# First layer's local attention: the second 128 queries in two halves with 128 keys each, two transposes a head, turned pairs in alternating PSUM banks

## The chip, the cores and the metric

The kernel runs on one core of one Trainium2 chip. The metric is the device time of one execution in microseconds (us). Before the change it is 3183.15 us, the median of 3 runs (3178.4 to 3184.4).

The core has a matrix engine (TensorE; PE in the rows, its weight loads PEld), a vector engine (VectorE, DVE), an activation engine (ScalarE, ACT), GpSimd (POOL) and a sync engine (SyncE, SP) that here issues the transfers. TensorE writes to PSUM, which has eight banks of 512 fp32 numbers in each of 128 partitions; everything else lies in SBUF.

## The reference

Two decoder layers over 8 sequences of 256 tokens with 512 features. Each layer has an attention (layer 0) or a state-space mixer (layer 1), a cross attention and a feed-forward block with experts. The change touches the local attention of layer 0 alone:

```python
q = q * cos + _rotate_half(q) * sin            # 16 heads of 32 features
k = k * cos + _rotate_half(k) * sin
scores = jnp.einsum('bhqd,bhkd->bhqk', q, k) * scale
rel = pos[:, None] - pos[None, :]
keep = (rel >= 0) & (rel < window)             # window is 64 for these constants
scores = jnp.where(keep[None, None], scores, -jnp.inf)
attn = jax.nn.softmax(scores, axis=-1)
out = jnp.einsum('bhqk,bhkd->bhqd', attn, v)
x = x + out.transpose(0, 2, 1, 3).reshape(B, S, EMB) @ w_out.T
```

A query sees itself and the 63 keys before it. Queries 0 to 127 need keys 0 to 127. Queries 128 to 191 need keys 65 to 191, and queries 192 to 255 need keys 129 to 255.

## The kernel before

`phase1` does the layer's two attentions, one sequence after the other (`for i in range(nseq)`). Each engine has one program, written out by hand, and it runs in the order in which it is written; engines wait for each other by semaphores (`due(name, i, k)` is the count of the k-th event of sequence i). There is no scheduler.

For a sequence, TensorE first computes queries and keys (`queries_keys`) and the values (`values(i, j)`, one for each 128 tokens j, into bank 6 + j). Then comes the stage that the change is about, here called the local stage. Heads go in pairs, n = 0 to 7, and a group c of four heads is two pairs. In program order TensorE does, for n = 0 to 11: `scores(i, n)` (n < 8), `values(i, 1)` (at n = 1), `turn_probs(i, n - 2)` (n = 2 to 9), and at n = 4, 6, 8, 10 `local_values` and `turn_recips` of group (n - 4) / 2. Right behind it stand `cross_values(0)` and the output projection.

- `scores` (L768 to L783): into two banks, one for each head of the pair, pair n using banks 0 and 1 or 2 and 3 in turn. First two bf16 matmuls lay the mask down (identity times `wmask_b`, 320 columns: 128 for the first 128 queries and `BAND` = 192 for the second); then the scores are added to it, 128 queries by keys 0 to 127 and 128 queries by keys 64 to 255. A head has 32 features, so the two heads lie on different 32-row strips of the array.
- VectorE takes the smallest (negated) score of each row for both blocks (L1047, L1048), ScalarE the exponentials with their row sums: for each head one of 128 and one of 192 columns (L669, L671), `scale=-1`, bias the smallest score. They go into `probs`, three buffers deep, where 64 zero columns lie between the two blocks.
- `turn_probs` (L785 to L794) transposes the pair's probabilities, 6 blocks of 128x128 (3 a head: queries 0 to 127 by keys 0 to 127, and queries 128 to 255 by keys 0 to 127 and 128 to 255), into bank 6 for one head and bank 7 for the other. From pair 1 on it waits until VectorE has copied the previous pair (`probsT_ready`), as every pair uses both banks; pair 0 waits until both value blocks have left those banks (`v_ready`).
- VectorE copies the 2 x 384 turned columns to `probsT` (L1055). `local_values` multiplies them with the values, four heads side by side on 32-column strips of the array: keys 0 to 127 with all 256 queries, then keys 128 to 255 with the second 128 queries, added. The reciprocals of the row sums are turned by `turn_recips`, copied by ScalarE (L619), and VectorE divides (L991).

SyncE's part in a sequence i >= 1 is, in its order: the value weights; the store of the sequence before (`normed_rows` and `mid`, 512 KB each, once VectorE has normalised its rows, which it does in the local stage at n = 2); the 2 MB of the cross-query weights (`load_unit(XQ)`); then those of the next sequence's queries.

Of the kernel before, what the change touches and what calls it, by code (L numbers as in the profile page):

```python
# [37 lines left out]
P = 128  # L38
# [16 lines left out]
BAND = S - P + WINDOW  # L55
# [26 lines left out]
wq_in w_hi w_lo slot_a slot_b colsT_lo hrT0_hi  # L82
# [251 lines left out]
def phase1(nc, sy, const, dr, held, nseq=NSEQ):  # L334
# [6 lines left out]
    with ExitStack() as ctx:  # L341
# [6 lines left out]
        wmask_b, ident_b = sb("wmask_b", [P, P + BAND], BF16), sb("ident_b", [P, P], BF16)  # L348
# [13 lines left out]
        wmask = arena[:, 2048:2048 + P + BAND]  # L362
# [4 lines left out]
        v, xv = sb("v", [P, NT, D]), held["xv"]  # L367
        probs = sb("probs", [P, 3, 2, P + S])
        probsT = arena[:, 0:3 * 2 * (P + S)].rearrange("p (b k s) -> p b k s", b=3, k=2)
# [75 lines left out]
        def _(sp):  # L445
# [11 lines left out]

            def load_raw(u, n, end, sem):
                first = raw_piece(u, n)
                sp.dma_start(first if end == n + 1 else flat[("w_sg", "w_su", "w_sd")[u]][:, n * D:end * D],  # L460
                             dr["w_units"][:, u, n * D:end * D]).then_inc(sy[sem], 16)
# [27 lines left out]
            for i in range(nseq):  # L489
                if i == 0:  # L490
                    for u in (K, V, XQ):
                        store_unit(u)
                else:
# [4 lines left out]
                    sp.wait_ge(sy["qk_proj"], due("qk_proj", i, 2 * KC))  # L498
                    load_unit(XQ)
# [34 lines left out]
        def _(pool):  # L534
            rstd_pool(pool, sy, norm_in(0), mv, ve, rstd, const["minus_half"])
            pool.memset(probs[:, :, :, P:P + WINDOW], 0.0).then_inc(sy["init1"], 1)
# [49 lines left out]
        def _(act):  # L586
# [65 lines left out]
            act.wait_ge(sy["init1"], 2)  # L652

            for i in range(nseq):
# [7 lines left out]
                for n in range(LPAIRS):  # L662
# [4 lines left out]
                    for k in range(2):  # L667
                        scores = bank_pair(2 * (n % 2))[:, k, :]
                        act.activation(probs[:, n % 3, k, 0:P], scores[:, 0:P], ACT.Exp, bias=smin[:, n, 0, k:k + 1],  # L669
                                       scale=-1.0, accum_out=ssum[:, c, 0, r + k:r + k + 1])  # L670
                        act.activation(probs[:, n % 3, k, P + WINDOW:P + S], scores[:, P:P + BAND], ACT.Exp,  # L671
                                       bias=smin[:, n, 1, k:k + 1], scale=-1.0,
# [40 lines left out]
        def _(pe):  # L713
# [54 lines left out]
            def scores(i, n):  # L768
# [27 lines left out]
            def local_values(i, c):  # L796
# [3 lines left out]
                for kt, (at, q0) in enumerate(((0, 0), (S, P))):  # L800
                    for r in range(HPC):
                        hh = c * HPC + r
                        n = hh // 2
                        ins = pe.matmul(bank(4 + c % 2)[r * HD:(r + 1) * HD, q0:S], v[:, kt, hh * HD:(hh + 1) * HD],
                                        probsT[:, n % 3, hh % 2, at:at + S - q0], start=(kt == 0), stop=(kt == 1),
# [58 lines left out]
            for i in range(nseq):  # L864
# [16 lines left out]
                if i == 0:  # L881
                    pe.wait_ge(sy["w1b_in"], n_late * 16)
                    pe.wait_ge(sy["ctx_in"], 16)
                    pe.wait_ge(sy["init1"], 2)
# [55 lines left out]
        def _(dve):  # L940
# [86 lines left out]
            for i in range(nseq):  # L1027
# [2465 lines left out]
```

## Time and profile before

| | |
|---|---|
| runs | 3183.15 us median (3178.4 to 3184.4) |
| profiled execution, its span | 3185.5 us (2.35 us above the median; no other time of its own is recorded) |
| TensorE matmuls busy | 2994.5 us, 94% |
| VectorE busy | 2329.6 us, 73% |
| ScalarE busy | 1588.2 us, 50% |
| GpSimd busy | 811.0 us, 25% |
| phase 1 (0 to 785 us): TensorE, VectorE, ScalarE busy | 712.58, 493.23, 283.75 us |
| the eight local stages, from the first mask to the first matmul behind the stage | 25.49 to 25.95 us each, 205.01 us in all |

A matmul's row holds its whole way through the array (a transpose of 128 columns reads 272 ns), and matmuls overlap: what one costs is the distance between the starts of two. Rows of the same line that follow each other are merged in the timeline (x6 are six instructions), and an fp32 matmul shows as two instructions, its two passes. "<-" names what ended the idle time ahead of a row.

### The profile page before, as it was taken

What the parts mean: (1) busy time and instruction counts of PE and PEld (TensorE: products, weight loads), DVE (VectorE), ACT (ScalarE), POOL (GpSimd) and SP (SyncE); (2) the same over time, 40 slices, a digit from 0 to 9 for tenths busy, and PEclk for the clock granted to TensorE, in tenths of its full rate; (3) what the DMA queues carried; (4) which work ended last, traced back from release to release, by engine and by line L of the source; (5) the groups of instructions that cost most, each with busy time, mean ns of one, the idle gap of its engine ahead of it and who ended that gap; (6) DMA issues with size and microseconds to landing.
All of it is one profiled execution on the core that took longest, in us unless ns stands there. A gap on an engine that the chain in (4) does not pass through costs nothing. (4 is left out here: it accounts for less than half of the span.)

```text
span 3185.5 us, 61039 instructions
## 1 busy us (share of the span) xinstructions
PE 2994.5 (94%) x22689; PEld 2409.3 (76%) x22689; DVE 2329.6 (73%) x4385; ACT 1588.2 (50%) x3643; POOL 811.0 (25%) x975
## 2 busy tenths in 40 slices
PE   7999999998999999999999959999999989999999
PEld 5665666665898888888888846767666678888888
DVE  5666666665875688888888767878785877777776
ACT  3333333334221455555555426666575766555555
POOL 1220221220664211111111063250603012222222
PEclk9999999999999999999999979999999999999999
DMA  6324323321231677777777741121200032222222
GB/s 271 112 87 167 133 106 120 117 83 47 82 95 34 199 246 238 251 238 250 242 241 247 245 144 57 58 87 35 80 25 31 18 131 79 76 77 74 76 77 70
DMA packets 145257, 401.85 MB, mean 126 GB/s; under 512 B 39232, under 2 KB 47936, under 8 KB 132240
## 3 DMA queue, kind: packets, MB, share of 16 engines
q1 hardware_dynamic: 106608, 323.30, 29.8%
q0 software_dynamic: 18976, 50.45, 5.5%
q10 hardware_dynamic: 19456, 25.18, 2.3%
q8 instruction: 140, 2.29, 0.3%
q14 instruction: 77, 0.63, 0.1%
HBM read 344.09 MB, written 54.76 MB: 125 GB/s over the span
## 5 line engine op out<-in xcount | busy, mean ns | idle before, releaser
L288 POOL DMA_INDIRECT hr<-normed_rows,idx x128 | 123.7, 966 | 634.5 <-PE psum L302 587.8
L3008 POOL TENSOR_TENSOR mixf<-act 128x256 f32<-128x256 f32 x128 | 143.2, 1119 | 458.3 <-DVE act L3274 458.3
L174 POOL TENSOR_SCALAR ve<-mv 128x1 f32<-128x1 f32 x112 | 35.8, 320 | 815.5 <-DVE mv L956 546.4
L328 PE MATMUL psum<-xT_hi,wgu_hi 128*128 128x192 f32 (+1 forms) x1536 | 227.9, 270 | 1.4 <-PEq L1117 0.8
L328 PE MATMUL psum<-xT_hi,wgu_lo 128*128 128x192 f32 (+1 forms) x1536 | 223.1, 267 | 0.0
L328 PE MATMUL psum<-xT_lo,wgu_hi 128*128 128x192 f32 (+1 forms) x1536 | 222.6, 267 | 0.0
L1734 ACT ACTIVATE eth<-psum 128x192 f32<-128x192 f32 (+1 forms) x192 | 63.2, 330 | 299.1 <-PE psum L328 294.3
L328 PEld LDWEIGHTS psum<-xT_hi,wgu_hi 128*128 128x128 f32 (+1 forms) x1536 | 189.8, 182 | 26.3 <-ACT wgu_hi L1718 21.5
L2302 ACT ACTIVATE scratch<-psum,smin 128x512 f32<-128x512 f32 x256 | 173.6, 686 | 59.9 <-DVE smin L2748 57.8
L328 PEld LDWEIGHTS psum<-xT_hi,wgu_lo 128*128 128x128 f32 (+1 forms) x1536 | 190.3, 182 | 0.0
L328 PEld LDWEIGHTS psum<-xT_lo,wgu_hi 128*128 128x128 f32 (+1 forms) x1536 | 190.2, 182 | 0.0
L2748 DVE TENSOR_REDUCE smin<-psum 128x2 f32<-128x1024 f32 x128 | 155.2, 1215 | 38.6 <-PE psum L2479 37.9
L3274 DVE TENSOR_TENSOR act<-act,maskT 128x512 f32<-128x512 f32 x128 | 88.1, 688 | 116.7 <-ACT act L3050 116.3
L2489 PEld LDWEIGHTS psum<-ident,scratch 128*128 128x128 f32 x1024 | 112.0, 143 | 56.7 <-issue 39.1
L2489 PE MATMUL psum<-ident,scratch 128*128 128x128 f32 x1024 | 148.0, 286 | 5.1 <-DVE scratch L2755 2.7
L1844 DVE SCALAR_TENSOR_TENSOR eact<-eth,psum 128x192 f32<-128x192 f32 (+1 forms) x192 | 67.4, 351 | 112.4 <-ACT eth L1734 110.0
L3284 DVE TENSOR_TENSOR ca_lo<-act,ca_hi 128x512 fp32r<-128x512 f32 x128 | 134.2, 1049 | 12.4
L1257 POOL DMA_INDIRECT slot_token<-tok_i,slot_w x96 | 105.8, 1102 | 66.7 <-DVE slot_r L1582 37.4
L723 PE MATMUL psum<-hT_hi,w_slot 128*128 128x256 f32 x768 | 111.3, 289 | 11.8 <-ACT hT_hi L600 5.9
L2116 POOL DMA_INDIRECT yk<-expert_out,slots x84 | 86.8, 1033 | 124.2 <-issue 49.5
L1088 DVE TENSOR_SCALAR arena<-psum,hi 128x512 f32<-128x512 f32 x128 | 87.5, 743 | 40.9 <-PE psum L826 40.8
L3063 ACT ACTIVATE ca_hi<-act 128x512 fp32r<-128x512 f32 x128 | 81.0, 633 | 66.5 <-DVE act L3274 66.5
(466 smaller groups left out, 8725.9 us busy)
## 6 DMA issues: line engine op xcount, KB each, us to landing
w_sg<-in_w_gu_dram SPq DMA_DIRECT2D x32, 1408.0 KB
w_su<-in_w_gu_dram SPq DMA_DIRECT2D x32, 1408.0 KB
w_slot<-w_split SPq DMA_DIRECT2D x21, 2048.0 KB
w_raw<-in_w_dram SPq DMA_DIRECT2D x128, 256.0 KB, 2.6
w_sd<-in_w_d_dram SPq DMA_DIRECT2D x32, 512.0 KB
wd<-in_w_d_dram SPq DMA_DIRECT2D x32, 512.0 KB
expert_out<-so ACTq DMA_DIRECT2D x64, 256.0 KB, 5.3
w_slot<-w_split SPq DMA_DIRECT2D x28, 512.0 KB
```

Source lines behind the costliest of these rows:

```text
L288: pool.indirect_dma_start(out=xg[0:w, t, :], out_offset=None, in_=rows, in_offset=bass.IndirectOffsetOnAxis(ap=idx[0:w, t:t + 1], axis=0)) ...
L328: ins = pe.matmul(bank(2 + m)[0:w, gu * CAP:(gu + 1) * CAP], wgu2[wp][:, gu, kc, m0:m0 + w], xT2[xp][:, kc, :], start=(i == 0 and kc == 0) ...
L723: ins = pe.matmul(out, lhs_of(lp, kc), rhs_of(rp, kc), start=(m == 0 and kc == 0), stop=(m == 2 and kc == KC - 1))
L1088: dve.tensor_scalar(xprobs[:, n % 4, kt], bank_pair(2 * (n % 2))[:, :, kt * S:(kt + 1) * S], hi[:, kt:kt + 1], -SCORE_CLIP * ROOT_HD, ALU. ...
L1257: pool.indirect_dma_start(out=dr["slot_token"], out_offset=bass.IndirectOffsetOnAxis(ap=slot_w[s % 2][:, j, k:k + 1], axis=0), in_=tok_i[s ...
L2116: pool.indirect_dma_start(out=gathered(s, NT * k + j), out_offset=None, in_=dr["expert_out"], in_offset=bass.IndirectOffsetOnAxis(ap=slots ...
L2302: act.activation(prob[:, q % 4, k, :], bank_pair(2 * (q % 2))[:, k, :], ACT.Exp, bias=smin[b][:, n, k:k + 1], scale=-1.0, accum_out=ssum[b ...
L2489: ins = pe.transpose(bank(4 + k)[:, mc * P:(mc + 1) * P], prob[:, q % 4, k, mc * P:(mc + 1) * P], ident)
L2748: dve.tensor_reduce(smin[(q // PAIRS) % 2][:, q % PAIRS, :], bank_pair(2 * (q % 2)), AX.X, ALU.min).then_inc(sy["smin_ready"], 1)
L3008: pool.tensor_tensor(mixf[:, g % LAG, :], act2[:, g % LAG, 0, :], act2[:, g % LAG, 1, :], ALU.add).then_inc(sy["f_mix"], 1)
L3274: dve.tensor_tensor(act2[:, g % LAG], act2[:, g % LAG], maskT[(g // FC) % 2][:, 2:4, :], ALU.mult).then_inc(sy["f_ca"], 1)
L3284: dve.tensor_tensor(ca2[1][:, g % LAG], act2[:, g % LAG], ca2[0][:, g % LAG].bitcast(F32), ALU.subtract).then_inc(sy["f_ca_lo"], 1)
```

## The change

The second 128 queries are taken in two halves. Queries 128 to 191 meet keys 64 to 191, queries 192 to 255 meet keys 128 to 255: 128 keys each, so that every row of scores has 128 columns in both blocks.

- Mask: 256 columns instead of 320. Scores: the second block's matmul of 128 queries by 192 keys becomes two of 64 queries by 128 keys, which write partitions 0 to 63 and 64 to 127 of the same columns (tile positions `(r0, 0)` and `(r0, 64)`).
- One reduction over both blocks instead of two; four exponentials of 128 columns a pair instead of two of 128 and two of 192. The zero columns in `probs` go.
- Four transposes a pair instead of six. Both heads of a pair fill one bank (6 for even pairs, 7 for odd), so `turn_probs` waits for the copy of the pair before last; pairs 0 and 1 wait for one value block each. The copy takes 512 columns instead of 768.
- `local_values`: per head one matmul of 128 columns and two of 64, nothing added. The middle half needs keys 64 to 191 on partitions 0 to 127, so SyncE copies the halves of two value blocks into a new tile `v_mid` (`shift_values`, two transfers of 64 rows of 2 KB within SBUF, once `v_ready` is complete). Group 0 waits for it (`vs_in`). In sequences 1 to 7 these transfers stand between the store and the cross-query weights, in sequence 0 ahead of the last weight store.

```diff
+            def shift_values(i):
+                sp.wait_ge(sy["v_ready"], due("v_ready", i, NT))
+                sp.dma_start(v_mid[0:HALF, :], v[HALF:P, 0, :]).then_inc(sy["vs_in"], 16)
+                sp.dma_start(v_mid[HALF:P, :], v[0:HALF, 1, :]).then_inc(sy["vs_in"], 16)
...
                     sp.wait_ge(sy["qk_proj"], due("qk_proj", i, 2 * KC))
+                    shift_values(i)
                     load_unit(XQ)
...
-                        act.activation(probs[:, n % 3, k, P + WINDOW:P + S], scores[:, P:P + BAND], ACT.Exp,
-                                       bias=smin[:, n, 1, k:k + 1], scale=-1.0,
+                        act.activation(probs[:, n % 3, k, P:S], scores[:, P:S], ACT.Exp,
+                                       bias=smin[:, n, k, 1:2], scale=-1.0,
...
-                    pe.matmul(bank_pair(2 * (n % 2))[:, k, 0:P + BAND], ident_b[:], wmask_b[:], start=True,
+                    pe.matmul(bank_pair(2 * (n % 2))[:, k, 0:S], ident_b[:], wmask_b[:], start=True,
                               stop=True)
                 c = n // 2
-                for q0, k0, at, width in ((0, 0, 0, P), (P, WINDOW, P, BAND)):
+                for p0, end, q0, k0, at in ((0, P, 0, 0, 0), (0, HALF, P, HALF, P), (HALF, P, P + HALF, P, P)):
                     for k in range(2):
-                        rows = slice((2 * (n % 2) + k) * HD, (2 * (n % 2) + k + 1) * HD)
-                        ins = pe.matmul(bank_pair(2 * (n % 2))[:, k, at:at + width], qk[rows, c, q0:q0 + P],
-                                        qk[rows, KC + c, k0:k0 + width], start=False, stop=True,
-                                        skip_group_check=True)
+                        r0 = (2 * (n % 2) + k) * HD
+                        rows = slice(r0, r0 + HD)
+                        ins = pe.matmul(bank_pair(2 * (n % 2))[p0:end, k, at:at + P], qk[rows, c, q0:q0 + end - p0],
+                                        qk[rows, KC + c, k0:k0 + P], start=False, stop=True,
+                                        tile_position=(r0, p0), skip_group_check=True)
...
-                if n >= 1:
-                    pe.wait_ge(sy["probsT_ready"], due("probsT_ready", i, n))
+                if n >= 2:
+                    pe.wait_ge(sy["probsT_ready"], due("probsT_ready", i, n - 1))
                 else:
-                    pe.wait_ge(sy["v_ready"], due("v_ready", i, NT))
+                    pe.wait_ge(sy["v_ready"], due("v_ready", i, n + 1))
                 for k in range(2):
-                    for b3 in range(3):
-                        ins = pe.transpose(bank(6 + k)[:, b3 * P:(b3 + 1) * P],
-                                           probs[:, n % 3, k, b3 * P:(b3 + 1) * P], ident)
+                    for t in range(NT):
+                        ins = pe.transpose(bank(6 + n % 2)[:, k * S + t * P:k * S + (t + 1) * P],
+                                           probs[:, n % 3, k, t * P:(t + 1) * P], ident)
...
+                if c == 0:
+                    pe.wait_ge(sy["vs_in"], 2 * 16 * (i + 1))
-                for kt, (at, q0) in enumerate(((0, 0), (S, P))):
+                for keys_of, q0, q1 in ((v[:, 0, :], 0, P), (v_mid[:], P, P + HALF), (v[:, 1, :], P + HALF, S)):
                     for r in range(HPC):
...
-                        dve.tensor_reduce(smin[:, n, 0, :], pair[:, :, 0:P], AX.X, ALU.min)
-                        dve.tensor_reduce(smin[:, n, 1, :], pair[:, :, P:P + BAND], AX.X, ALU.min
-                                          ).then_inc(sy["lmin_ready"], 1)
+                        dve.tensor_reduce(smin[:, n], pair[:, :, 0:S].rearrange("p k (t s) -> p k t s", t=NT), AX.X,
+                                          ALU.min).then_inc(sy["lmin_ready"], 1)
...
-                        dve.tensor_copy(probsT[:, m % 3], bank_pair(6)[:, :, 0:P + S]
+                        dve.tensor_copy(probsT[:, m % 3].rearrange("p k s -> p (k s)"), bank(6 + m % 2)
                                         ).then_inc(sy["probsT_ready"], 1)
```

On TensorE, before, from the scores of pair 4 to those of pair 5 (`wmask_b` is the mask, `qk` the scores, `probs` the transposes, `arena,v` the values, `recb` the reciprocals):

```order
L773 MATMUL psum<-wmask_b,ident_b 128x320 x2
L779 MATMUL psum<-qk 128x128 x2
L779 MATMUL psum<-qk 128x192 x2
L792 MATMUL psum<-ident,probs 128x128 x6
L804 MATMUL psum<-arena,v 32x256 x4
L804 MATMUL psum<-arena,v 32x128 x4
L812 MATMUL psum<-ident,recb 128x128 x2
L773 MATMUL psum<-wmask_b,ident_b 128x320 x2
L779 MATMUL psum<-qk 128x128 x2
```

The same place after the change:

```order
L779 MATMUL psum<-wmask_b,ident_b 128x256 x2
L786 MATMUL psum<-qk 128x128 x2
L786 MATMUL psum<-qk 64x128 x4
L799 MATMUL psum<-ident,probs 128x128 x4
L813 MATMUL psum<-arena,v 32x128 x4
L813 MATMUL psum<-arena,v_mid 32x64 x4
L813 MATMUL psum<-arena,v 32x64 x4
L821 MATMUL psum<-ident,recb 128x128 x2
L779 MATMUL psum<-wmask_b,ident_b 128x256 x2
L786 MATMUL psum<-qk 128x128 x2
```

The steps stand in the same order; two transposes and 64 mask columns are gone, the second scores are four matmuls on 64 output partitions, and the values are twelve matmuls with fewer columns.

On SyncE's queue, before, in sequence 2 (`w_slot_76` and `w_slot_77` are the two weight slots, `so` holds the rows stored):

```order
L468 DMA w_slot_76<-w_split 128x1024 x4
L455 DMA normed_rows<-so 128x2x512
L456 DMA mid<-so 128x1024
L468 DMA w_slot_77<-w_split 128x4096
L468 DMA w_slot_76<-w_split 128x4096
```

The same place after the change:

```order
L473 DMA w_slot_76<-w_split 128x1024 x4
L455 DMA normed_rows<-so 128x2x512
L456 DMA mid<-so 128x1024
L460 DMA v_mid<-v 64x512
L461 DMA v_mid<-v 64x512
L473 DMA w_slot_77<-w_split 128x4096
L473 DMA w_slot_76<-w_split 128x4096
```

The two new transfers stand behind the store's 1 MB and ahead of 4 MB of weights.

## Rows read from the trace of the kernel before

**Rows 1.** Busy time by stretch: sequence 2's local stage, and all eight

```profile
core 0: us, PE busy (x) PEld busy (x) DVE busy (x) ACT busy (x) POOL busy (x), PEclk, DMA share, GB/s
239.89:265.49 25.60, 22.65 (x213) 15.16 (x213) 19.64 (x40) 14.19 (x68) 0.19 (x1) 1.00 0.53 207
...
sum 205.01, PE 181.15 PEld 121.24 DVE 156.40 ACT 117.05 POOL 1.34; mean PE 22.64 PEld 15.15 DVE 19.55 ACT 14.63 POOL 0.17
```

**Rows 2.** Timeline of TensorE, sequence 2 (start, length, engine, line, operation, count, idle before)

```profile
246.63 0.85 PE L792 MATMUL psum<-ident,probs 128*128 128x128 f32 x6 [0.39 <-ACT v L613]
...
251.18 0.27 PE L792 MATMUL psum<-ident,probs 128*128 128x128 f32 x1
251.38 0.42 PE L804 MATMUL psum<-arena,v 128*32 128x256 f32 x4
251.38 0.86 PE L804 MATMUL psum<-arena,v 128*32 128x256 f32 x16
...
252.44 0.43 PE L773 MATMUL psum<-wmask_b,ident_b 128*128 128x320 bf16 x2
252.81 0.82 PE L779 MATMUL psum<-qk 32*128 32x128 f32 x8
253.56 0.87 PE L792 MATMUL psum<-ident,probs 128*128 128x128 f32 x6
254.27 0.43 PE L773 MATMUL psum<-wmask_b,ident_b 128*128 128x320 bf16 x2
...
256.35 0.86 PE L804 MATMUL psum<-arena,v 128*32 128x256 f32 x16
...
261.31 0.86 PE L804 MATMUL psum<-arena,v 128*32 128x256 f32 x16
```

**Rows 3.** Groups by line and shape in phase 1 (busy us, mean ns of one)

```profile
L1047 DVE TENSOR_REDUCE lmin<-psum 128x2 f32<-128x256 f32 x64 | 26.9, 420 | 35.5 <-PE psum L779 35.0
L1048 DVE TENSOR_REDUCE lmin<-psum 128x2 f32<-128x384 f32 x64 | 35.0, 547 | 0.0
L1055 DVE COPY arena<-psum 128x768 f32<-128x768 f32 x64 | 60.9, 951 | 13.7 <-PE psum L792 13.1
L1088 DVE TENSOR_SCALAR arena<-psum,hi 128x512 f32<-128x512 f32 x128 | 87.5, 743 | 40.9 <-PE psum L826 40.8
L669 ACT ACTIVATE probs<-psum,lmin 128x128 f32<-128x128 f32 x128 | 47.1, 368 | 60.3 <-DVE lmin L1048 60.1
L671 ACT ACTIVATE probs<-psum,lmin 128x192 f32<-128x192 f32 x128 | 54.0, 421 | 0.0
```

**Rows 4.** Timeline of ScalarE: first and last exponential of pair 5

```profile
254.59 0.37 ACT L669 ACTIVATE probs<-psum,lmin 128x128 f32<-128x128 f32 x1 [1.26 <-DVE lmin L1048]
...
255.99 0.21 ACT L671 ACTIVATION_READ_ACCUMULATOR probs<-psum,lmin 128x1 f32 x1
```

**Rows 5.** Groups by line and shape: weight loads of 128, 64 and 32 columns

```profile
L779 PEld LDWEIGHTS psum<-qk 32*128 32x128 f32 x64 | 4.2, 185 | 2.1 <-issue 2.1
L1791 PEld LDWEIGHTS psum<-wd,eact 128*64 128x64 f32 x12 | 0.8, 136 | 0.7 <-issue 0.4
L804 PEld LDWEIGHTS psum<-arena,v 128*32 128x32 f32 x512 | 13.4, 109 | 19.8 <-DVE arena L1055 10.3 <-issue 4.0
```

**Rows 6.** Sequence 2: the store's issue, its transfers to landing, the last value copy

```profile
244.58 0.37 SPq L455 DMA_DIRECT2D normed_rows<-so  x1
...
normed_rows<-so SPq DMA_DIRECT2D x1, 512.0 KB, 2.8
mid<-so SPq DMA_DIRECT2D x1, 512.0 KB, 4.1
...
245.85 0.63 ACT L613 ACTIVATE v<-psum 128x512 f32<-128x512 f32 x1
```

**Rows 7.** Busy time by stretch, layer 1: ahead of and in a stretch at half clock

```profile
2020.00:2028.00 8.00, 6.30 (x68) 4.05 (x65) 7.96 (x13) 5.22 (x14) 0.80 (x2) 1.00 0.01 3
2028.00:2038.00 10.00, 9.51 (x76) 6.95 (x80) 7.14 (x12) 4.31 (x12) 1.58 (x4) 0.50 0.00 0
```

More of the change, by code:

```diff
@@ L54 @@
 NEG = -1e30
-BAND = S - P + WINDOW
+HALF = P // 2
 LPAIRS = HEADS // 2
@@ L81 @@
 xattn_ready delta_psum delta_taken clip_bounds rs_ready shared_in init1 x_in ctx_in mask_in rows_out
-wq_in w_hi w_lo slot_a slot_b colsT_lo hrT0_hi
+wq_in w_hi w_lo vs_in slot_a slot_b colsT_lo hrT0_hi
 """.split()
@@ L347, in phase1 @@
         cosT, sinT = sb("cosT", [P, S]), sb("sinT", [P, S])
-        wmask_b, ident_b = sb("wmask_b", [P, P + BAND], BF16), sb("ident_b", [P, P], BF16)
+        wmask_b, ident_b = sb("wmask_b", [P, S], BF16), sb("ident_b", [P, P], BF16)
         bq, bk = sb("bq", [P, KC]), sb("bk", [P, KC])
@@ L361, in phase1 @@
         qk_raw = arena[:, 0:2 * KC * S].rearrange("p (c s) -> p c s", c=2 * KC)
-        wmask = arena[:, 2048:2048 + P + BAND]
+        wmask = arena[:, 2048:2048 + S]
         qk = sb("qk", [P, 2 * KC, S])
@@ L366, in phase1 @@
         swap = [p ^ 1 for p in range(HD)]
-        v, xv = sb("v", [P, NT, D]), held["xv"]
-        probs = sb("probs", [P, 3, 2, P + S])
-        probsT = arena[:, 0:3 * 2 * (P + S)].rearrange("p (b k s) -> p b k s", b=3, k=2)
+        v, v_mid, xv = sb("v", [P, NT, D]), sb("v_mid", [P, D]), held["xv"]
+        probs = sb("probs", [P, 3, 2, S])
+        probsT = arena[:, 0:3 * 2 * S].rearrange("p (b k s) -> p b k s", b=3, k=2)
         smin, ssum = sb("lmin", [P, LPAIRS, 2, 2]), sb("lsums", [P, KC, NT, HPC])
@@ L490, in _ @@
                 if i == 0:
-                    for u in (K, V, XQ):
+                    for u in (K, V):
                         store_unit(u)
+                    shift_values(0)
+                    store_unit(XQ)
                 else:
@@ L535, in _ @@
             rstd_pool(pool, sy, norm_in(0), mv, ve, rstd, const["minus_half"])
-            pool.memset(probs[:, :, :, P:P + WINDOW], 0.0).then_inc(sy["init1"], 1)
             sy.link(pool, "pool_link", pool.memset(one_hot[:], 0.0))
@@ L651, in _ @@
             cols_copy(turned_in(0))
-            act.wait_ge(sy["init1"], 2)
             for i in range(nseq):
@@ L668, in _ @@
                         scores = bank_pair(2 * (n % 2))[:, k, :]
-                        act.activation(probs[:, n % 3, k, 0:P], scores[:, 0:P], ACT.Exp, bias=smin[:, n, 0, k:k + 1],
+                        act.activation(probs[:, n % 3, k, 0:P], scores[:, 0:P], ACT.Exp, bias=smin[:, n, k, 0:1],
                                        scale=-1.0, accum_out=ssum[:, c, 0, r + k:r + k + 1])
-                        act.activation(probs[:, n % 3, k, P + WINDOW:P + S], scores[:, P:P + BAND], ACT.Exp,
-                                       bias=smin[:, n, 1, k:k + 1], scale=-1.0,
+                        act.activation(probs[:, n % 3, k, P:S], scores[:, P:S], ACT.Exp,
+                                       bias=smin[:, n, k, 1:2], scale=-1.0,
                                        accum_out=ssum[:, c, 1, r + k:r + k + 1]).then_inc(sy["probs_ready"], 1)
@@ L803, in local_values @@
                         n = hh // 2
-                        ins = pe.matmul(bank(4 + c % 2)[r * HD:(r + 1) * HD, q0:S], v[:, kt, hh * HD:(hh + 1) * HD],
-                                        probsT[:, n % 3, hh % 2, at:at + S - q0], start=(kt == 0), stop=(kt == 1),
+                        ins = pe.matmul(bank(4 + c % 2)[r * HD:(r + 1) * HD, q0:q1], keys_of[:, hh * HD:(hh + 1) * HD],
+                                        probsT[:, n % 3, hh % 2, q0:q1], start=True, stop=True,
                                         tile_position=(0, r * HD), skip_group_check=True)
@@ L883, in _ @@
                     pe.wait_ge(sy["ctx_in"], 16)
-                    pe.wait_ge(sy["init1"], 2)
+                    pe.wait_ge(sy["init1"], 1)
                     keys(0, range(KC))
@@ L3432, in host_layout @@
     q, k = np.arange(P)[:, None], np.arange(P)[None, :]
-    k1 = np.arange(WINDOW, S)[None, :]
+    k1 = np.where(q < HALF, k + HALF, k + P)
     keep = np.concatenate([(q >= k) & (q - k < WINDOW), (q + P >= k1) & (q + P - k1 < WINDOW)], 1)
```

## The prediction

> **What bounds the kernel now.** I read the busy time by stretch first. The eight local stages take 205.0 us of the 3185.5, each about 25.6, and in one of them no engine is full: of 25.60 us TensorE shows 22.65, VectorE 19.64, ScalarE 14.19 [rows 1]. So the stage is a chain that goes round between the engines, and the timeline of TensorE shows the ring. From one group's values to the next (251.38 to 256.35) are 4.97 us [rows 2]. TensorE's own steps in it, start to start: values and reciprocals 1.06 (251.38 to 252.44), scores 1.12 (252.44 to 253.56) and six transposes 0.71 (253.56 to 254.27), the last two twice: 4.72 us. The other 0.25 us is waiting for VectorE's copy, because every pair of heads uses both turned banks. So TensorE bounds the middle of the stage, VectorE and ScalarE its opening and its end, where there are no other scores to fill in.
>
> What the stage gives up reaches the end: the matmuls of cross values follow it at once and need nothing of it, and the profile shows no transfer that this part of phase 1 waits for.
>
> **The change part by part, on TensorE.**
>
> - Transposes: six take 0.87 us to the last one's end and one takes 0.27, so 0.12 us from start to start [rows 2]; two fewer turn the step's 0.71 us into 0.49.
> - Mask: two matmuls of 320 columns and one change of the array's tiling take 0.37 us (252.44 to 252.81) [rows 2]. The change of tiling is about 0.1: from the last transpose to the first values matmul are 0.20 us (251.18 to 251.38), of which 0.11 is the transpose's own streaming [rows 2]. So 0.13 us for 320 columns, 0.11 for 256: 0.05 us saved on two.
> - Scores: eight instructions in 0.75 us (252.81 to 253.56) [rows 2]. With 0.11 us for a pass of 128 columns and 0.16 for 192 these are two passes of each (0.54), a first weight load that nothing hides (0.11) and the change of tiling behind (0.1). After: two passes of 128 (0.22), another change of tiling, from 32x128 to 32x64 tiles (0.1), a load that is not hidden (0.05: the load of 64 columns takes 136 ns, between 185 for 128 and 109 for 32 [rows 5]), and, if the two halves run side by side, two passes of 128 (0.22) with 0.02 for issuing four tiles. With the first load and the last change as before that is 0.82 us, 0.07 more than before, and the mask gives 0.05 back. The step stays at 1.12 us: fewer columns, one more change. Bounds: 0.97 us if that change costs nothing, 1.33 if the halves run one after the other.
> - Values: before, passes of 256 and of 128 columns twice each, 0.64 us. After, two of 128 and four of 64: 0.44 if a pass of 64 costs half of one of 128, 0.66 if it costs as much. No row here has 64 columns on 32-column strips. I take 0.44, because what could hold a short pass up is its weight load, and that is the shortest one here [rows 5]: values and reciprocals 1.06 to 0.86 us.
>
> **On the other engines.** VectorE's two reductions take 420 ns (256 elements) and 547 (384), 1 ns an element; one of 512 is 0.67 us in place of 0.97. The copy of 768 takes 951 ns, of 512 by the same slope 0.69; the nearest row, another instruction on 512 columns, has 743 [rows 3]. ScalarE's four exponentials run from 254.59 to 256.20, 1.61 us [rows 4]; two get shorter by 421 less 368 ns [rows 3], so 1.50.
>
> **The walk through one stage** (sequence 2), with hand-overs between engines of about 0.1 us:
>
> - First mask to first values, 11.49 us before. Two pairs of scores, the second value block and the third scores are as they were. Pair 0's transposes no longer wait for the second value copy (0.39 us [rows 2]) and start at 246.2. The scores of pair 4 then wait for the exponentials of pair 2: 246.2 + 0.67 + 1.50 and hand-overs, 248.6. Adding 1.12 and 0.49, the values start at 250.2: 10.34 us.
> - First to second values: TensorE alone, 0.86 + 2 x (1.12 + 0.49) = 4.08 in place of 4.97. The copies are ready in time, because a pair now has a bank of its own.
> - Second to third values, 4.96 before (256.35 to 261.31): scores of pair 7 end 2.05 us after the start; reduction, copy and hand-overs add 1.45: 3.50. VectorE sets this.
> - Third values to the stage's end, 4.18 before (261.31 to 265.49): pair 7's transposes wait for its exponentials (0.94), then 0.63 to their end, copy 0.69, hand-overs 0.18, values and reciprocals 0.86: 3.30.
>
> Together 4.38 us. With before's durations the same walk comes out 0.2 short of the rows, so I count 4.2. Eight stages: 33.6 us. From the profiled execution's 3185.5 that is 3151.9; it lies 2.35 above the median, and from the median it is 3149.6.
>
> **The added wait.** Group 0's values wait for `v_mid`; behind them on TensorE stand the reciprocals and all later scores, and for those both other engines wait. The second value copy ends at 246.48 (245.85 + 0.63) [rows 6], about 0.5 us earlier after the change; two issues at 0.37 us follow. The store's transfers of 512 KB took 2.8 and 4.1 us from issue to landing [rows 6], the second behind the first. `v_mid` has 256 KB and queues behind that store, so 248.8 to 250.5 us against a need at 250.2: I cost it at nothing, with up to 0.3 us a stage. The cover is the opening; past it each us late is a us lost. The cross-query weights are moved behind it by about 1.4 us, and the output projection and more stand ahead of their first use.
>
> **A page's rule against the change.** The four column tiles of the values start together: four matmuls in 0.42 us, while their rows are 0.39 long [rows 2], all on the same 128 rows. The Trainium skill, in "TensorE: Matmul & The Clock Gate", Part 3 (what overlaps and what doesn't), says that a weight load overlaps running matmuls only when the row groups differ. By that rule the two halves of a head, which share their rows, would run one after the other, and the time would be the first rival's; the trace disagrees for 32-column tiles, and no run here shows 64-column tiles on 32 rows.
>
> **The rivals.**
>
> 1. The halves run one after the other: 0.21 us more for each of seven scores that TensorE waits for nothing else in, 1.5 a stage, 12 in all: 3162. For it: no row mixes row and column tiles. Against: each alone runs side by side [rows 2].
> 2. The third tiling costs no change: scores 0.97, about 1.3 us a stage more saved, 10.5 in all: 3139. "TensorEngine Tiling (Array Packing)", Key Properties, of the Trainium skill says that changing the tiling mode drains the engine; by it this rival falls, but no row shows these two modes side by side.
> 3. `v_mid` comes late. If its small packets are served mixed with the weights behind them (2 MB, at up to twice the stretch's mean 207 GB/s [rows 1] 5 us), it lands near 253.3, 3.1 us late in sequences 1 to 7: 22 lost, 3172. Against: the store's two transfers landed one after the other.
> 4. Slower: TensorE's clock falls in the stage. It is at 2.4 GHz in all eight [rows 1]. In layer 1 it fell to half for 10 us behind 8 us with 6.30 busy [rows 7], and the new stage streams fewer columns with more gaps. One such stretch in every stage doubles 5 us of steps: 8 x (5 - 4.2) = 6 us lost, 3190. It decides from 8.4 us at 1.2 GHz a stage; all of it would be far worse, above 3300. Against: TensorE's share of the stage hardly falls (4.08 of 4.08 in the middle).
> 5. The change doesn't do what it says: the new bank order still makes pairs wait, 0.5 us a stage: 3154, inside the forecast's own range.
>
> **How the numbers follow.** Forecast 0.67 (rival 5 in it), own range 3144 to 3156 (values not shorter costs 0.7 us a stage, a copy of 743 ns a little). Rival 1 0.12, rival 2 0.10, rival 3 0.06, rival 4 0.05. The range reaches over both tiling rivals, 3138 to 3164, and leaves out most of 3 and 4. About 0.2%, 6.4 us, is what a measurement of this kernel can tell from no change. Faster: 0.67 + 0.12 + 0.10 and half of rival 3, 0.92; same 0.04; slower 0.04, nearly all rival 4.
>
> **What would show it.** In the profile after: stages near 21.3 us; distance from first to second values near 4.1; the scores' second block starting about 0.4 us behind the first, its four matmuls within 0.03 us (right) or 0.2 apart (rival 1); 64-column passes 0.06 apart; one reduction of 0.67 and a copy of 0.69; no idle TensorE ahead of the first values; granted clock 1.00. The prediction is wrong if that first wait is over 1 us, or the clock row shows halves in a stage.

## The result, and the profile after

The changed kernel takes 3152.55 us, the median of 4 runs (3145.23 to 3157.93), beside 3183.78 us (3178.4 to 3188.07) for the kernel before on the same chip: 0.9906 of its time, 95% interval 0.989 to 0.9922, or 31.2 us less. The profiled execution has a span of 3156.0 us, 29.5 less than before's 3185.5. The forecast was 3150, with 33.6 us saved in the eight local stages. The total is near that; what the profile saves in the stages is not. Of six later runs of the changed kernel (below) one took 6928.04 us; nothing on record says why, and it is left out of every comparison.

The busy time by stretch for the eight local stages of the changed kernel, which answers to [rows 1] (columns as there; the granted clock, PEclk, is the third from the end, 1.00 being 2.4 GHz):

```profile
41.95:63.59 21.64, 20.07 (x261) 13.58 (x261) 15.24 (x31) 15.75 (x73) 0.00 (x0) 0.99 0.48 190
141.12:162.41 21.29, 19.86 (x260) 13.53 (x261) 15.85 (x32) 13.12 (x68) 0.19 (x1) 1.00 0.67 262
232.07:253.36 21.29, 19.86 (x260) 13.53 (x261) 15.84 (x32) 13.13 (x68) 0.19 (x1) 1.00 0.67 261
323.04:345.87 22.83, 21.41 (x261) 14.66 (x261) 15.84 (x32) 13.23 (x68) 0.19 (x1) 0.93 0.64 243
415.53:438.34 22.81, 21.39 (x261) 14.63 (x261) 15.85 (x32) 13.24 (x68) 0.19 (x1) 0.93 0.64 243
508.00:530.77 22.77, 21.34 (x260) 14.55 (x261) 15.85 (x32) 13.24 (x68) 0.19 (x1) 0.93 0.65 244
600.48:628.24 27.76, 25.65 (x260) 17.33 (x261) 16.12 (x32) 13.34 (x68) 0.19 (x1) 0.75 0.51 200
697.90:719.20 21.30, 19.88 (x261) 13.53 (x262) 15.83 (x32) 13.12 (x68) 0.19 (x1) 1.00 0.44 161
sum 181.69, PE 169.46 PEld 115.34 DVE 126.42 ACT 108.18 POOL 1.34; mean PE 21.18 PEld 14.42 DVE 15.80 ACT 13.52 POOL 0.17
```

Where the granted clock is 1.00 and nothing is late, here called an undisturbed stage, it takes 21.29 us in place of 25.60, 4.31 less. Sequences 3, 4 and 5 are 1.5 us longer at a mean clock of 0.93, and sequence 6 is 6.5 us longer at 0.75. So the stages save 205.01 - 181.69 = 23.3 us in this execution. All eight without those losses (7 x 21.29, and 21.64 for sequence 0) would take 170.7 and save 34.3.

The other 6.2 us of the span's 29.5 lie in layer 1, whose code is the same. Two stretches of it, each from the same matmul to the same matmul, before and after:

```profile
1800.10:2000.00 199.90, 157.15 (x1115) 116.93 (x1114) 141.65 (x272) 93.93 (x246) 86.42 (x110) 0.91 0.37 120
2200.00:2400.00 200.00, 189.07 (x1603) 139.17 (x1604) 153.47 (x278) 126.23 (x330) 63.75 (x91) 0.96 0.20 59
```

```profile
1776.70:1973.30 196.60, 157.20 (x1115) 117.22 (x1114) 142.73 (x272) 93.69 (x246) 86.07 (x110) 0.90 0.38 122
2173.30:2369.70 196.40, 185.96 (x1604) 136.71 (x1605) 153.59 (x278) 126.17 (x330) 64.08 (x92) 0.97 0.19 60
```

They are 3.3 and 3.6 us shorter after. In the second a higher granted clock goes with it (0.97 for 0.96); in the first none does, and the cause there is open. Such differences come from execution to execution: the four runs above lie 12.7 us apart. From the first matmul behind phase 1 (transposes of `hr`) to the end are 2419.8 us before and 2413.4 after in these two profiles, and 2409.0 and 2409.6 in a second profile of each kernel (below, taken on two different chips). In that second pair the span is 31.1 us shorter, all of it in phase 1, which ends 31.8 us earlier.

An undisturbed stage, sequence 2 from the first to the last local values, on the timeline of TensorE (columns as in [rows 2], to which it answers):

```profile
242.53 0.43 PE L813 MATMUL psum<-arena,v 128*32 128x128 f32 x8
242.77 0.29 PE L813 MATMUL psum<-arena,v_mid 128*32 128x64 f32 x8
242.88 0.29 PE L813 MATMUL psum<-arena,v 128*32 128x64 f32 x8
243.11 0.44 PE L821 MATMUL psum<-ident,recb 128*128 128x128 f32 x2
243.38 0.38 PE L779 MATMUL psum<-wmask_b,ident_b 128*128 128x256 bf16 x2
243.69 0.87 PE L786 MATMUL psum<-qk 32*128 32x128 f32 x12
244.49 0.66 PE L799 MATMUL psum<-ident,probs 128*128 128x128 f32 x4
244.99 0.38 PE L779 MATMUL psum<-wmask_b,ident_b 128*128 128x256 bf16 x2
...
246.68 0.42 PE L813 MATMUL psum<-arena,v 128*32 128x128 f32 x8
...
248.65 1.09 PE L799 MATMUL psum<-ident,probs 128*128 128x128 f32 x8
250.13 0.42 PE L813 MATMUL psum<-arena,v 128*32 128x128 f32 x8 [0.39 <-DVE arena L1063]
...
251.07 0.66 PE L799 MATMUL psum<-ident,probs 128*128 128x128 f32 x4
252.51 0.43 PE L813 MATMUL psum<-arena,v 128*32 128x128 f32 x8 [0.78 <-DVE arena L1063]
```

From one group's values to the next are 4.15 us (242.53 to 246.68), with no idle TensorE between them; before it was 4.97. Values and reciprocals take 0.85 (242.53 to 243.38), the scores step 1.11 (243.38 to 244.49), the transposes 0.50 (244.49 to 244.99). TensorE still waits for VectorE's copy ahead of the last two groups, 0.39 and 0.78 us.

VectorE's and ScalarE's instructions, groups by line and shape in phase 1, which answer to [rows 3]:

```profile
L675 ACT ACTIVATE probs<-psum,lmin 128x128 f32<-128x128 f32 x128 | 47.5, 371 | 56.4 <-DVE lmin L1056 55.7
L1063 DVE COPY arena<-psum 128x512 f32<-128x512 f32 x64 | 43.7, 683 | 1.8 <-PE psum L799 1.7
L1056 DVE TENSOR_REDUCE lmin<-psum 128x4 f32<-128x512 f32 x64 | 43.5, 688 | 54.7 <-PE psum L786 54.7
```

**The clock in sequences 3 to 5.** Sequence 3's opening (from the first mask to the first values) on TensorE, and then the same eight matmuls of the second value block in sequence 2:

```profile
321.05 1.09 PE L729 MATMUL psum<-w_slot,hT_lo 128*128 128x512 f32 x4
323.04 0.38 PE L779 MATMUL psum<-wmask_b,ident_b 128*128 128x256 bf16 x2 [0.90 <-DVE qk L960]
323.35 0.87 PE L786 MATMUL psum<-qk 32*128 32x128 f32 x12
...
325.27 3.62 PE L729 MATMUL psum<-w_slot,hT_hi 128*128 128x512 f32 x8
```

```profile
234.30 2.12 PE L729 MATMUL psum<-w_slot,hT_hi 128*128 128x512 f32 x8
```

TensorE idles 0.90 us for VectorE's rotated queries (L960), runs two pairs of scores, and then eight matmuls of the second value block last 3.62 us, in place of 2.12 in sequence 2: the granted clock is at half, 1.2 GHz, for 3.4 us from 325.49. Sequences 4 and 5 show the same (3.59 and 3.36 us). Such a stretch in an opening is called a fall below.

**The wait in sequence 6.** TensorE there:

```profile
612.08 0.59 PE L813 MATMUL psum<-arena,v 128*32 128x128 f32 x8 [1.07 <-DMA v_mid<-v]
```

It waits 1.07 us for `v_mid`, and from there the clock is at half, as the stretch behind it shows:

```profile
612.20:625.80 13.60, 13.60 (x135) 9.28 (x132) 6.07 (x13) 5.58 (x30) 0.00 (x0) 0.50 0.55 233
```

In sequence 2 `v_mid`'s second transfer is issued at 238.84 and its last part lands 2.93 us later, 0.76 ahead of the values. In sequence 6 it is 4.70 us: 30 of the 32 parts have landed by 610.29, the last two at 611.58 and 611.95. The queues' packets from the first issue on, for 5.3 us: in sequence 6 this line beside the one of queue 1, in sequence 2 queue 1 alone (queue, kind: packets, MB, share of the 16 engines):

```profile
q8 instruction: 1, 0.02, 1.1%
```

```profile
q1 hardware_dynamic: 440, 1.86, 101.1%
```

In sequence 6 one 16 KB packet of instructions is moved in that time, in sequence 2 none.

### The profile page after: what moved, and what is told of

Same layout as the page of the kernel before. It is cut to its first block and busy times, and to the rows that moved or that the text cites. A ratio compares the mean times of both kernels' runs of the same rounds, so it can differ in the third digit from the quotient of the medians.

```text
span 3156.0 us, 61772 instructions
## 1 busy us (share of the span) xinstructions
PE 2980.2 (94%) x23073; PEld 2400.3 (76%) x23073; DVE 2302.3 (73%) x4321; ACT 1579.9 (50%) x3643; POOL 809.4 (26%) x974
```

## The experiments

Theory A: the mechanism is the one forecast, 4.3 us a stage, and what is missing is lost to a clock that falls behind idle time in the thinner openings, and to a `v_mid` that lands with less than 1 us to spare. Against it: that the bank order, the tiling or `v_mid` costs something everywhere; or that the clock falls by chance, in the kernel before as well. Times of single runs stand beside the kernel before on the same chip: 3179.35 us (one run) for the first four, 3186.23 (median of 11) for the changed kernel once more and the last three, 3184.64 (one run) for the kernel before and the two second runs; stages and intervals are from the profiles. A single run doesn't tell two of these kernels apart by its time: the changed kernel's own runs lie up to 12.7 us apart.

**Both heads' turned probabilities in both banks again**

```diff
-                if n >= 2:
-                    pe.wait_ge(sy["probsT_ready"], due("probsT_ready", i, n - 1))
+                if n >= 1:
+                    pe.wait_ge(sy["probsT_ready"], due("probsT_ready", i, n))
...
-                        ins = pe.transpose(bank(6 + n % 2)[:, k * S + t * P:k * S + (t + 1) * P],
+                        ins = pe.transpose(bank(6 + k)[:, t * P:(t + 1) * P],
...
```

> The changed kernel with the old bank order: a pair's heads in banks 6 and 7, each pair waiting for the copy of the one before. Theory (the walk of the prediction): a stage at full clock goes from 21.3 us to about 21.8, 0.5 us more, because TensorE's own steps still cover most of the wait: 4 us in all. Rival: the bank order is what removed the wait of 0.25 us a pair of iterations and also the waits at both ends, so undoing it costs 1 us a stage or more (22.3 or over). Second rival: it costs nothing (21.3).

Measured: 3159.01 us; stages 21.92 in six of sequences 1 to 7. First values (10.46) and the middle (4.15) are unchanged, although pair 0 waits for both value blocks again and each pair for the one before it; the third interval is 4.09 in place of 3.45:

```profile
250.78 0.66 PE L799 MATMUL psum<-ident,probs 128*128 128x128 f32 x4
252.35 0.63 PE L799 MATMUL psum<-ident,probs 128*128 128x128 f32 x4 [0.92 <-DVE arena L1063]
```

Two pairs' transposes stand next to each other there, and the second now waits 0.92 us for the copy of the first. The alternating banks are worth 0.63 us a stage, and only at the end. In the middle the copy is out in time either way: the 0.82 us that an interval there gained came from the shorter steps and not from the bank order.

**The second 128 queries in one piece**

```diff
-                for p0, end, q0, k0, at in ((0, P, 0, 0, 0), (0, HALF, P, HALF, P), (HALF, P, P + HALF, P, P)):
+                for p0, end, q0, k0, at in ((0, P, 0, 0, 0), (0, P, P, HALF, P)):
```

> The second 128 queries meet keys 64 to 191 in one matmul of 128 queries instead of two of 64, so the last 64 queries are scored against the wrong keys; all else as in the changed kernel. It has the same columns and no third tiling. Theory: the change of tiling from 32x128 to 32x64 costs about 0.15 us in each scores step (1.11 us becomes 0.96) and a full-clock stage goes from 21.3 to about 20.0 us. Rival: the change of tiling is hidden behind the waits for the other engines, and the stage stays within 0.3 us of 21.3.

> The kernel that takes the second 128 queries in one matmul against keys 64 to 191, once more (wrong scores for queries 192 to 255). It has the 0.86 us of idle time ahead of the first scores and had no fall in seven openings. Theory A1 (the four tiles of 64 columns are part of what makes the clock fall): no fall again. Theory A2 (the idle time alone does, and the first profile had luck): one to four falls in the openings of sequences 1 to 7, 1.5 us each. In either case first values about 0.14 us behind v_mid's last part in the undisturbed stages.

Measured: 3135.81 us at first, with undisturbed stages of 20.19, 1.10 less; a second time 3150.98 (before: 3184.64). The middle is 3.85 in place of 4.15, so the four tiles of 64 columns cost 0.15 us a scores step over one matmul of 128. That is as forecast for the third tiling (0.15). First values come at 9.83, and `v_mid`'s last part lands 0.14 us ahead of that in every stage but the one with a fall, the same distance as where TensorE is seen waiting for it: here it is already the bound of the opening. In three stages it was late: 1.68 us in sequence 3 of the second run, with an instruction packet between the second issue and the landing, and 1.02 and 0.53 us in sequence 3 of the first run and sequence 1 of the second. In these two the packet came earlier and SyncE's issue of the first half, which it overlapped, took 1.56 and 1.21 us in place of 0.47:

```profile
325.20 1.56 SPq L460 DMA_DIRECT2D v_mid<-v  x1
```

Of the clock, the second run decides for A2: a fall in sequence 5's opening, none in the first run. The 64-column tiles are not needed for it.

**Four thrown-away matmuls in the idle time ahead of the first scores**

```diff
+                if i >= 1:
+                    pe.wait_ge(sy["delta_taken"], due("delta_taken", i - 1, NT))
+                    for kc in range(KC):
+                        pe.matmul(bank(7)[:, :], hT2[0][:, kc, P:2 * P], w_slot[0][:, kc, 0, :], start=True, stop=True)
```

> In sequences 1 to 7 four more matmuls of 128x512 run ahead of the first scores, in the 0.9 us in which TensorE waits for the rotated queries; their result is overwritten. Nothing gets shorter by it. Theory: the clock fell to 1.2 GHz in the second value block of sequences 3, 4 and 5 of the changed kernel because the idle 0.9 us and the thinner scores ahead of it left TensorE too idle; with the extra work these stages run at full clock, about 21.3 us as in sequences 1, 2 and 7, and no stretch at half clock starts in the opening of a stage. Rival: whether the clock falls depends only on where the stage happens to lie, and falls are as frequent as before (three of seven openings).

> The kernel with four thrown-away matmuls in the idle time ahead of the first scores, once more. Theory A (the filled idle time keeps the clock up): no fall in the openings of sequences 1 to 7, now 28 openings of filled kernels without one. Rival (luck): at least one fall. For v_mid: late by more than 1 us only in a stage where a 16 KB instruction packet is moved between its issue and its landing.

Measured: 3147.24 and 3151.73 us. In 14 openings no fall. The first run from its first mask to behind its last stage, at a granted clock of 1.00:

```profile
41.80:748.00 706.20, 671.01 (x5561) 457.76 (x5560) 439.43 (x758) 261.23 (x800) 134.08 (x184) 1.00 0.34 121
```

The stages take 21.30 to 21.32, except sequence 3's, 22.20 in the first run (0.81 us of waiting ahead of the first values, with an instruction packet between `v_mid`'s issue and its landing) and 21.62 in the second (0.32 us more in the second group's values; the cause is open). Work without use, put into the idle time, costs the stage 0.01 to 0.03 us and keeps the clock up.

**No middle tile: no transfers and no wait**

```diff
-                    shift_values(i)
...
-                if c == 0:
-                    pe.wait_ge(sy["vs_in"], 2 * 16 * (i + 1))
-                for keys_of, q0, q1 in ((v[:, 0, :], 0, P), (v_mid[:], P, P + HALF), (v[:, 1, :], P + HALF, S)):
+                for keys_of, q0, q1 in ((v[:, 0, :], 0, P), (v[:, 0, :], P, P + HALF), (v[:, 1, :], P + HALF, S)):
```

> No middle value tile: the two transfers and the wait for them are gone, and the middle half multiplies with the first value block (wrong values for queries 128 to 191). Theory: in a full-clock stage the transfers land about 0.7 us before they are needed, so those stages stay at 21.3 us, and only a stage like sequence 6 of the changed kernel, where one transfer was 1.07 us late and the clock fell right after that wait, gets shorter: no stretch at half clock starts at the first values. Falls of the clock in the second value block may stay. Rival: the added wait costs something in every stage, and all of them get shorter by 0.3 us or more.

Measured: 3152.97 us; undisturbed stages 21.29, first values at 10.45. So in an undisturbed stage `v_mid` costs nothing. The clock still falls in four openings (sequences 3, 4, 6, 7), sequence 3's as in the changed kernel:

```profile
322.99 0.38 PE L777 MATMUL psum<-wmask_b,ident_b 128*128 128x256 bf16 x2 [0.84 <-DVE qk L956]
...
325.21 3.67 PE L727 MATMUL psum<-w_slot,hT_hi 128*128 128x512 f32 x8
```

The transfers have no part in those falls.

**The changed kernel and the kernel before once more**

> The changed kernel once more, unaltered, on the chip of the next three. Theory A (what is left out of the forecast's 4.2 us a stage is the clock, which falls by chance in the openings behind the 0.9 us in which TensorE waits for the rotated queries): undisturbed stages 21.3 again, stages with a fall 22.8, but not necessarily the same sequences as in the first profile; time 3145 to 3158. Theory B (the falls and the wait for v_mid in sequence 6 belong to fixed places of the program): falls in sequences 3, 4, 5 and the wait in 6 once more.

> The kernel before once more, on the chip of the next two, for its granted clock. Theory A (the clock falls in the openings only since the change, because what TensorE does there has become thinner): no stretch at half clock inside a local stage of sequences 1 to 7, first values 11.49 us behind the first mask in each. Rival (the falls come by chance in the kernel before as well, and its first profile had luck): at least one stage with a fall, 1.5 us longer.

Measured, changed kernel: five of six runs at 3147.54 to 3156.1 us, 0.9892 of before (0.9875 to 0.991). Falls in sequences 3 and 4, 22.8 us each, not in 5; the wait for `v_mid` again in sequence 6, 1.14 us, with an instruction packet again in its window, this time without a long stretch at half clock behind it. Theory B holds for the wait: the packet comes 8.6 us behind sequence 6's first mask in both profiles. For the falls neither holds whole. Sequence 5's did not come again, but sequences 3 and 4 fall in both profiles here, without the middle tile and with the early `v_mid` (below), and every fall in an opening begins 1.7 to 2.8 us behind the first mask. So which opening falls is not chance alone; it goes with where the opening lies in the run, and the openings of one profile are not independent trials.

Kernel before: 3178.81 us, no fall in the stages of sequences 1 to 7 (25.60 to 25.95 us), as in its first profile; sequence 0's has 3.4 us at half clock near its end (27.09). The waits of TensorE ahead of the first scores in phase 1 (total us, times, longest), in the first and second profile of the kernel before and then of the changed one:

```profile
PE psum L773 <- DVE qk L951: 5.3, 6, 1.2
PE psum L773 <- DVE qk L951: 3.9, 6, 1.0
PE psum L779 <- DVE qk L960: 6.5, 7, 1.2
PE psum L779 <- DVE qk L960: 7.3, 7, 1.3
```

The kernel before idles there too, but less: 0.09 to 1.19 us, and 0.74 or more in 8 of 14 stages.

**`v_mid` ahead of the store, its first half as soon as the first value block is there**

```diff
             def shift_values(i):
-                sp.wait_ge(sy["v_ready"], due("v_ready", i, NT))
+                sp.wait_ge(sy["v_ready"], due("v_ready", i, 1))
                 sp.dma_start(v_mid[0:HALF, :], v[HALF:P, 0, :]).then_inc(sy["vs_in"], 16)
+                sp.wait_ge(sy["v_ready"], due("v_ready", i, NT))
```

and the call moved ahead of the store.

> The first half of v_mid is copied as soon as the first value block is there, the second as soon as the second is, both ahead of the store's 1 MB. Theory A (v_mid lands about 0.7 us ahead of its need, and one late packet or one slow issue is enough to lose that): v_mid lands at least 1.5 us earlier against the stage's start, TensorE waits for it in no sequence, undisturbed stages stay at 21.3; the store goes out 1 us later and nothing waits for that; time as the changed kernel's within 5 us. Rival (the late packets come whatever lies ahead of them in the queue): a wait of about 1 us for v_mid in at least one stage again.

Measured: 3157.84 us. In sequences 1 and 2 `v_mid`'s last part lands 8.5 us behind the first mask, 1.2 us earlier (1.5 were expected), and TensorE waits for it nowhere, in sequence 6 neither, where an instruction packet again delayed it (9.17). The clock falls in four openings (3, 4, 5, 7), and the time is no better (the changed kernel's five: 3147.54 to 3156.1): this cures the wait alone.

**A third of the second value block ahead of the first scores**

```diff
+                if i >= 1:
+                    values(i, 1, 0, 1)
...
-                        values(i, 1)
+                        values(i, 1, 1 if i >= 1 else 0, 3)
```

> In sequences 1 to 7 the first of the three products of the second value block (four matmuls, about 1.05 us) is moved ahead of the first scores, into the 0.9 us in which TensorE waits for the rotated queries. Theory A (that idle time ahead of thinner work lets the clock fall, and it is TensorE that sets the opening): no stretch at half clock in an opening; the distance from stage to stage goes from 90.95 to about 90.0; with the clock losses gone about 10 us under the changed kernel's profile, span near 3143 to 3147. Rival B (ScalarE's exponentials set the opening): distance stays within 0.2 of 90.95, the gain is the falls alone, 5 us. Rival C (the falls have nothing to do with the idle time): falls in openings as before, 1.5 us each.

Measured: 3146.39 us, span 3144.4. That is 11.6 under the changed kernel's first profile but only 1.3 under its second, on the same chip: from one run no gain in the total is shown. No fall in any opening. From stage to stage are 90.24 to 90.43 us in place of 90.95, 0.6 less and not 1.0: between A and B. Sequence 2's opening shows why:

```profile
230.08 1.09 PE L729 MATMUL psum<-w_slot,hT_hi 128*128 128x512 f32 x4
231.00 0.39 PE L782 MATMUL psum<-wmask_b,ident_b 128*128 128x256 bf16 x2
...
235.53 0.38 PE L782 MATMUL psum<-wmask_b,ident_b 128*128 128x256 bf16 x2 [0.15 <-ACT probs L677]
```

The idle time is filled, but TensorE now waits 0.15 us for ScalarE's exponentials at the third scores, beside the 0.26 at the fifth that the changed kernel has too, and `v_mid` lands 0.14 us ahead of the first values, the distance at which it is waited for.

**All of it: early `v_mid`, filled opening, filled end**

```diff
+                    if i >= 1 and n == LPAIRS + 2:
+                        cross_values(0, 0, 1)
...
-                cross_values(0)
+                cross_values(0, 1 if i >= 1 else 0)
```

beside the edits of the last two.

> Both of the last two, and one matmul of the cross values moved ahead of the last local values, into the 0.78 us in which TensorE waits for the last copy of turned probabilities. Theory A: 1.0 us a stage at the opening, 0.3 (one matmul of 512 columns) at the end, no falls of the clock in openings and no wait for v_mid: 7 x 1.3 = 9 us under an undisturbed run of the changed kernel, and 5 to 10 more than that under a run with falls: 3135 to 3142. Rival: the clock falls elsewhere instead, or another engine sets the opening: 3146 or more, less than 5 us under the changed kernel on the same chip.

Measured: 3136.01 us, the median of 5 runs (3130.38 to 3137.74), 0.9838 of before (0.9821 to 0.9855). Every run is below every run of the changed kernel on the same chip; the medians of five lie 14.8 us apart. From stage to stage are 89.4 us, 1.5 less than in the changed kernel. 1.3 were expected, 1.0 at the opening and 0.3 at the end; what came is 0.6 and 0.9. With `v_mid` 1.2 us ahead of the first values these come at 9.85, so `v_mid` no longer bounds this opening: TensorE waits for the exponentials up to twice a stage, 14 times and 3.0 us in all. No fall in an opening; 0.2 us of waiting for `v_mid` in sequence 6, where an instruction packet fell between its issue and its landing once more. The end of sequence 2's stage:

```profile
249.10 0.66 PE L803 MATMUL psum<-ident,probs 128*128 128x128 f32 x4
249.59 1.02 PE L831 MATMUL psum<-w_xv,ctxT 128*128 128x512 f32 x2
250.54 0.43 PE L817 MATMUL psum<-arena,v 128*32 128x128 f32 x8
```

One fp32 matmul of 512 columns is two instructions and fills 0.95 us, from 249.59 to 250.54; where the changed kernel waits 0.78 for the copy, nothing is left to wait for.

## Why the prediction was right, and where it was not

**Right: the walk through the stage.** In an undisturbed stage the four intervals are 10.45, 4.15, 3.45 and 3.23 us, 21.29 in all, for a walk of 10.34, 4.08, 3.50 and 3.30. The walk saved 4.38, 4.2 were counted, 4.31 were measured. Each operation came out within 0.03 us: scores 1.11 (1.12), transposes 0.50 (0.49), values and reciprocals 0.85 (0.86), reduction 0.69 (0.67), copy 0.68 (0.69). One reason in it was wrong: that the copies are ready in time in the middle "because a pair now has a bank of its own". With the old bank order the middle is 4.15 us as well.

**Rivals 1 and 2 fell.** The twelve scores of a pair take 0.80 us (243.69 to 244.49). One after the other the halves would add 0.21, and single records show the four tiles of a pass starting within 0.02 us. So in this case tiles on the same 32 rows run side by side. That is against the rule as the prediction read it in the Trainium skill ("TensorE: Matmul & The Clock Gate", Part 3). The third tiling costs 0.15 us a scores step against one piece, as the sum had it; the run with one piece shows the four tiles as a whole, not the change of mode by itself.

**Rival 5 fell.** The new bank order does what it says, and without it 0.63 us a stage would be gone, all in the third interval.

**Failed: the step that saw the clock at 1.00, and rival 4's form.** The prediction named the mechanism and gave it 5 in 100, as one 10 us stretch in every stage. What came was 3.4 us at half clock in the openings of some sequences, at 1.5 us each. The idle time ahead of the scores is needed for it. With it left in, the kernels with the thinner stage (the changed kernel twice, the ones with the old banks, without the middle tile, with the early `v_mid`) show it in 14 of 35 openings. With that time filled it is 0 of 28, and the place alone doesn't explain that: sequence 3 of the first run with thrown-away matmuls starts at 322.57 us, 0.4 ahead of where it starts and falls without the middle tile (322.99). That the thinner work is needed too is not shown. The kernel before has 0 of 14, but it idles less; with 0.7 us or more of idle time it is 0 of 8, beside 14 of 33 in those five profiles. And the two runs in one piece, thinner still, have 1 of 14. What picks the openings among those that idle is open as well: those that fall come behind 0.72 to 1.41 us of it, those that don't behind 0.54 to 1.27.

**Mis-sized: the wait for `v_mid`.** "At nothing, with up to 0.3 us a stage" was right for the undisturbed stages (0.76 us to spare, and taking the wait away gained nothing). It missed that the slack is less than one delay of the queue. Over the ten profiles that have `v_mid`, in sequences 1 to 7, a 16 KB instruction packet lies between the second transfer's issue and its landing in 9 of 70 stages, and in these 9 that takes 0.4 to 1.8 us longer than in the same kernel's undisturbed stages. In four of them TensorE waits 0.8 to 1.7 us, in the others the clock's fall or an earlier issue covers it or leaves 0.2. In two more stages, both of the kernel in one piece, the packet comes a little earlier, the issue is long, and TensorE waits 0.5 and 1.0 us. Twice, in the changed kernel's sequence 6 and in the second run with one piece, 13.7 us at half clock follow the wait, which cost another 5.4 and 5.5. The Trainium skill, in "DMA: Bandwidth & Descriptors" (Arbitration), says that each DMA engine takes turns between the queues, a packet at a time; the rows fit it, in that the two late parts in sequence 6 landed at 611.58 and 611.95, behind that packet's end at 610.03. Which of the 16 engines moved which packet no run here shows.

**Right in total partly by luck.** The forecast's 33.6 us are the stages' 34.3 without losses. The profile lost 11.0 of them (1.5 three times, 6.5 once) and got 6.2 back in layer 1, where nothing was changed. That run was the slowest of its four, 5.4 us above their median. In the second pair of profiles luck plays less: the eight stages save 31.9 us, and the span is 31.1 shorter.

## What to carry to other kernels

A step shortened by a walk over start-to-start distances comes out as the walk says, if the resource that binds each interval is named; each interval was within about 2% here. What such a walk leaves out is the engine's clock: where work that was made thinner follows idle time, look at the granted clock there, and whether useful work from further down can be moved into that gap. It paid twice here, by the work moved and by the clock. A transfer that lands less than 1 us ahead of its need is not hidden: in 6 of 70 stages it came 0.5 to 1.7 us too late here, each time near a packet of instructions. Issuing it ahead of the store left the undisturbed stages at 21.29 to 21.30 us.

## What the runs showed of the hardware

- Four score tiles of 64 columns, two on each of two 32-row strips of the array, start within 0.02 us of each other; the values with 64 columns on 32-column strips follow at 0.056 us a pass (two passes in the 0.11 from 242.77 to 242.88), half of what 128 columns take.
- Instruction packets of 16 KB are moved beside the data by DMA, 0.9 to 1.7 us each, 42 to 44 of them in phase 1 of the kernels with the change. A transfer of 128 KB with one between its issue and its landing lands 0.4 to 1.8 us late, and the four issues of `v_mid` on SyncE that overlapped one took 1.2 to 1.7 us in place of 0.5 to 0.6.
- Half the clock for 3.4 us cost 1.5 us in an opening. Ahead of the same place, matmuls whose results are thrown away cost the stage 0.01 to 0.03 us and kept the clock at 1.00 in 14 openings.
